# A decoder layer on one core: batches outermost and unrolled, with projection, norms and feed-forward placed between the attention steps

## The chip, the cores and the metric

One core of a Trainium2 chip, one launch. The metric is device time in microseconds from start to end of an execution, as the median of several runs. Beside it stands the span of one profiled execution, from its first to its last instruction.

## The reference

Four batches of 256 tokens, 256 channels, 16 heads of 128, float32. Three blocks follow one another, each with a residual and a layer norm without weights:

```python
q, k, v = x @ Wq, x @ Wk, x @ Wv                  # (4, 256, 16, 128) each
q, k = rmsnorm(q) * q_w, rmsnorm(k) * k_w
s = q k^T / sqrt(128) - slope[h] * (i - j)        # causal, slope[h] = 2 ** (-(h + 1) / 2)
y = rmsnorm(softmax(s) @ v) * sub_w               # per head
x = layernorm(x + concat(y) @ Wproj)              # (2048, 256)

a = softmax((ctx @ Wq.T + bq) (ctx @ Wk.T + bk)^T)  # (4, 256, 256), ctx has 128 channels
x = layernorm(x + x @ a^T)                        # over the channels of x

h = sigmoid(Q(x) @ Tg^T) * (Q(x) @ Tu^T)          # Tg, Tu, Td: ternary weights times their mean
x = layernorm(x + Q(h) @ Td^T)                    # Q: 8 bits per token; width 1024
```

## The kernel before

The tokens stand in tiles of 128, two per batch, eight in all (`NT`). Each engine runs its own list of instructions, and semaphores order them against one another; an engine never passes a waiting instruction of its own. The order of the work is written out by hand, the same way on each engine.

Prologue. SyncE issues all loads (L232 to L245). TensorE turns the cross-attention weights, the context and x, projects context queries and keys (L396) and forms the energies (L405). ScalarE and VectorE split the turned x into a high and a low part (`xT_hi` L596, `xT_lo` L720), so that three single-pass matmuls give a full-precision product. GpSimd does the same to the weights of the first two heads (`split`, L272 to L280: `w_hi` and `w_lo`, three pieces of 256 columns).

Attention. `attention_steps` (L206) runs 64 steps, one head of one batch in each, batches innermost: eight unrolled, then a loop of seven trips of eight (`Fori`). The weights of a head are therefore loaded and split once and used for four steps. A step works on several heads at once, as a pipeline: QKV of step n for tile 0 (L482), transposes of q and k of n-1 (L493), transposes of the probabilities of n-2 (L499), QKV of tile 1, scores of n-1 (L505, L506), values of n-2 (L512 to L514), transposes of y of n-3 (L521). The chain of one tile goes from QKV to squares (ScalarE, L635), sums (VectorE, L797), power -1/2 (GpSimd, L315), norm (VectorE, L791) and the transposes. QKV writes one PSUM bank per tile, so the next QKV of a tile waits for its norm. In some steps a piece of feed-forward weights is made ternary (`quantise_ff`, L777 to L782) and turned (L462), and in steps 3 to 6 the cross attention of a batch is normed and turned (L449). The turned y of all 64 heads stays in `yT`.

Tail. Only then the heads are projected: `project` (L422) accumulates 16 heads of a tile. The first two tiles fill the gaps of the last steps (`project_early`), the others those of a loop over tiles (L535 on), which does for a tile: residual and norm (L876), transposes (L550), cross attention (L557), norm, 8-bit quantisation (L900 to L904), gate and up (L587), sigmoid (L703), product (L865), quantisation of the hidden (L886 to L895, ScalarE L694), transposes (L564), down (L572), residual and norm (L908), store. Two neighbouring tiles overlap.

Of the kernel before, what the change touches and what calls it, by code (L numbers as in the profile page):

```python
# [40 lines left out]

def decoder_kernel(nc, x, ctx_in, wq, wk, wv, wproj, q_rms, k_rms, subln, xwq, xbq, xwk, xbk,
# [23 lines left out]
    ctx = ExitStack()
    with ctx:
# [3 lines left out]
        def sem(name):  # L71
# [6 lines left out]
        w_raw = sb("w_raw", [P, 2, KC, 3, D])  # L78
        w_hi = sb("w_hi", [P, 2, KC * 3 * D], F32R)
        w_lo = sb("w_lo", [P, 2, KC * 3 * D], F32R)  # L80
        bias = sb("bias", [P, 2, 3 * P])
        wp = sb("wp", [P, H, C])
        yT = sb("yT", [P, STEPS, T])
# [17 lines left out]
        v_sb = sb("v_sb", [P, B, TT, VW])  # L101
        y_n = sb("y_n", [P, TT, D])


        prep = yT[:].rearrange("p n t -> p (n t)")
        ctx_sb = prep[:, 0:NT * CC].rearrange("p (n c) -> p n c", n=NT)
        ctxT = prep[:, 1024:1024 + B * T]
        qcT = prep[:, 2048:2048 + B * T]
        kcT = prep[:, 3072:3072 + B * T]
        xw_sb = prep[:, 4096:4096 + 2 * CC].rearrange("p (a c) -> p a c", a=2)  # L110
        xwT = prep[:, 4352:4352 + 2 * CC].rearrange("p (a c) -> p a c", a=2)
        attn_sum = prep[:, 4608:4608 + NT]
        abs_w = prep[:, 5120:5120 + F]
        attn_raw = prep[:, 11264:11264 + NT * T].rearrange("p (n t) -> p n t", n=NT)
        attn = sb("attn", [P, NT, T])
        neg_xmax = sb("neg_xmax", [P, NT])
# [4 lines left out]
        ff_round = sb("ff_round", [P, C])  # L121
        ff_q = sb("ff_q", [P, C], BF16)
        w_sum = sb("w_sum", [P, 6])
        w_total = sb("w_total", [P, 3])
        w_scale = sb("w_scale", [P, 3])
        w_inv = sb("w_inv", [P, 3])


        res = sb("res", [P, 3, C])
        stats = sb("stats", [P, 3, nc.vector.BN_STATS_DIM])  # L130
        mean_var = sb("mean_var", [P, 3, 2])
        var_eps = sb("var_eps", [P, 3])
        ln_rstd = sb("ln_rstd", [P, 3])
        x1 = sb("x1", [P, C])
# [3 lines left out]
        x_most, x_scale, x_inv, h_most, h_scale, h_inv, down_scale = (sb(n, [P, 1]) for n in (  # L138
            "x_most", "x_scale", "x_inv", "h_most", "h_scale", "h_inv", "down_scale"))
        gate_up_scale = sb("gate_up_scale", [P, 2])  # L140
        round_col, table = sb("round_col", [P, 1]), sb("table", [P, 1])
        x_round = sb("x_round", [P, C])
        xq = sb("xq", [P, C], BF16)
        xqT = sb("xqT", [P, KC, P], BF16)

        sig, hid, h_round = ff_raw[:, 0, 0:F], ff_raw[:, 0, F:2 * F], ff_raw[:, 1, 0:F]
        hq = sb("hq", [P, F], BF16)
        hT = sb("hT", [P, FC, P], BF16)

# [7 lines left out]
        ps_yT = ps[:, 6, 0:T]  # L157
# [3 lines left out]
        s_vec, s_ctx, s_xw, s_wp = (sem(n) for n in ("vecs_loaded", "ctx_loaded", "xw_loaded", "wp_loaded"))  # L161
        s_ff = [sem("w_gate_loaded"), sem("w_up_loaded"), sem("w_down_loaded")]
        s_wraw = [sem("w_raw_even_loaded"), sem("w_raw_odd_loaded")]
        s_const, s_split_hi, s_split, s_bias, s_vecs = (sem(n) for n in (
            "constants_set", "w_hi_split", "w_lo_split", "bias_set", "vecs_scaled"))
        s_xT, s_xhi, s_xlo = sem("x_turned"), sem("xT_hi_set"), sem("xT_lo_set")
        s_cp = [sem("ctx_queries_projected"), sem("ctx_keys_projected")]
        s_ct, s_ctc, s_qcb, s_kcb, s_en, s_xmax, s_xexp, s_attn = (sem(n) for n in (
            "ctx_turned", "ctxT_copied", "ctx_queries_biased", "ctx_keys_biased", "energies_done", "energies_max",
            "energies_exp", "cross_attention_set"))  # L170
        s_at, s_atc = sem("cross_attention_turned"), sem("cross_attention_copied")
        s_wabs_act = sem("ff_abs_summed_by_scalar")
        s_wabs, s_wsum, s_wsc, s_wr, s_wq, s_wt, s_wtc = (sem(n) for n in (
            "ff_abs_summed", "ff_abs_total", "ff_scales_set", "ff_rounded", "ff_quantised", "ff_turned", "ff_turned_copied"))
# [7 lines left out]
        s_tqk, s_qkT, s_s, s_sc, s_p, s_tp, s_pT, s_y, s_sqy, s_ssy, s_yn, s_ty, s_yT = (sem(n) for n in (  # L182
            "qk_turned", "qkT_copied", "scores_done", "scores_biased", "probs_done", "probs_turned",
            "pT_copied", "y_done", "y_squared", "y_summed", "y_normed", "y_turned", "yT_copied"))
# [3 lines left out]
        (s_o, s_t1, s_x1T, s_xm, s_xq, s_gus, s_tq, s_xqT, s_gate, s_up, s_sig, s_hid, s_hs, s_hr, s_hq, s_th, s_hT,  # L188
         s_dn) = (sem(n) for n in (
             "projected", "x1_turned", "x1T_copied", "cross_mixed", "x2_quantised", "gate_up_scale_set", "xq_turned",  # L190
             "xqT_copied", "gate_done", "up_done", "sigmoid_done", "hidden_done", "hidden_scale_set",
             "hidden_rounded", "hidden_quantised", "hidden_turned", "hT_copied", "down_done"))
# [8 lines left out]
        def wait(eng, semaphore, count):  # L201

            if not isinstance(count, int) or count > 0:
                eng.wait_ge(semaphore, count)

        def attention_steps(eng, step, depth):  # L206

            for j in range(PAIR):  # L210
                step(j, j // B, j, lambda k, n=j: n >= k, 0)
            with eng.Fori(1, TRIPS) as trip:
                for j in range(PAIR):
                    step(trip * PAIR + j, trip * 2 + j // B, j, lambda k: True, trip)
            for n in range(STEPS, STEPS + depth):
                step(n, n // B, n % PAIR, lambda k, n=n: n - k < STEPS, TRIPS)

# [4 lines left out]
        def _(sp):  # L222
            def load_w(h, r):
                for a in range(3):
                    sp.dma_start(w_raw[:, r, :, a, :], w_d[a][:, :, bass.ds(h * D, D)]).then_inc(s_wraw[r], 16)
# [5 lines left out]

            sp.dma_start(xw_sb[:, 0, :], xwq).then_inc(s_xw, 16)  # L232
            sp.dma_start(xw_sb[:, 1, :], xwk).then_inc(s_xw, 16)
            sp.dma_start(ctx_sb, ctx_in.rearrange("b (t p) c -> p (b t) c", p=P)).then_inc(s_ctx, 16)
            for n, (first, last) in enumerate(((0, 1), (1, B))):
                tiles = slice(TT * first, TT * last)
                sp.dma_start(x_sb[:, tiles, :], x_d[:, tiles, :]).then_inc(s_x[n], 16)
            load_w(0, 0)
            for n, v in ((3, xbq), (4, xbk), (0, q_rms), (1, k_rms), (2, subln)):
                sp.dma_start(vecs[:, n:n + 1], v.rearrange("(p a) -> p a", a=1)).then_inc(s_vec, 16)  # L240
            load_w(1, 1)
# [466 lines left out]
        def _(dve):  # L708
# [75 lines left out]
            def step(n, head, j, live, trip):  # L784
# [22 lines left out]
                if live(0):  # L807
                    sums(0)
# [124 lines left out]
```

## Time and profile before

| | us |
|---|---|
| median of 3 runs | 435.16 (434.38 to 435.76) |
| span of the profiled execution | 432.9 |
| TensorE matmul busy | 401.9 (93%) |
| TensorE weight load busy | 361.1 (83%) |
| VectorE busy | 327.7 (76%) |
| ScalarE busy | 254.4 (59%) |
| GpSimd busy | 220.2 (51%) |

The end of a matmul is modelled in these records, and matmuls overlap, so a busy TensorE is no measure of its pace: for that the starts of successive groups are to be compared. The share of an engine is a mean over stages that have different limits. An idle time in front of an instruction is put down to what released it.

### The profile page before, as it was taken

The numbers are of one execution on the slowest core, as the hardware profiler recorded it, in microseconds if no ns is written. First come the engines' busy times: TensorE is split into PE (matmuls) and PEld (weight loads), VectorE is DVE, ScalarE is ACT, GpSimd is POOL, SyncE is SP. The second block draws the span as 40 slices with busy tenths as digits, with TensorE's granted clock in tenths as the row PEclk, the third lists the DMA queues.
The fourth block names the chain that finished last, engine by engine and source line by source line (L and its number), as shares of the span: only waits on it lengthen the run. The fifth ranks groups of instructions, "written<-read, shape, count | busy, mean of one in ns | idle before, by whom it ended". The sixth has DMA issues, their size and how long they took to land.

```text
span 432.9 us, 9595 instructions
## 1 busy us (share of the span) xinstructions
PE 401.9 (93%) x2605; PEld 361.1 (83%) x2612; DVE 327.7 (76%) x1000; ACT 254.4 (59%) x750; POOL 220.2 (51%) x368
## 2 busy tenths in 40 slices
PE   4979999999999999999999999999999899999552
PEld 3668899999999999999999999999988677777321
DVE  0777987887797798788779779878822788888862
ACT  3486777677676776767767677676722333333321
POOL 3633667676675776767767677675501122222210
PEclk9999999999999999999999999999999999999965
DMA  8980010110101101011010110000000000000000
GB/s 223 316 251 2 2 36 3 38 37 0 36 0 36 36 0 36 0 36 36 0 36 0 36 36 0 0 0 0 0 2 0 2 0 15 12 14 12 13 14 24
DMA packets 21747, 14.52 MB, mean 34 GB/s; under 512 B 1760, under 2 KB 21472, under 8 KB 21728
## 3 DMA queue, kind: packets, MB, share of 16 engines
q1 hardware_dynamic: 21728, 14.29, 11.2%
q8 instruction: 9, 0.15, 0.2%
q14 instruction: 10, 0.08, 0.1%
HBM read 13.24 MB, written 1.05 MB: 33 GB/s over the span
## 4 chain that ended last, share of the span: by engine, by line
PE 86%; DVE 5%; ACT 4%; issue 2%; DMA 1%; POOL 1%; SPq 0%; POOLq 0%; DVEq 0%
PE ps L482 30%; PE ps L422 11%; PE ps L493 7%; PE ps L506 6%; PE ps L499 5%; PE ps L512 4%; PE ps L505 3%; PE ps L514 3%; PE ps L513 3%; PE ps L521 3%; PE ps L587 3%; PE ps L572 2%; ACT hT L696 2%; DMA x_sb<-in_x 1%; PE ps L557 1%
## 5 line engine op out<-in xcount | busy, mean ns | idle before, releaser
L315 POOL TENSOR_TENSOR qk_rstd<-qk_sum,minus_half 128x2 f32<-128x2 f32 x128 | 88.5, 692 | 92.6 <-DVE qk_sum L797 90.8
L482 PE MATMUL ps<-w_hi,xT_hi 128*128 128x384 f32 x256 | 96.9, 378 | 2.3 <-DVE qk_n L791 1.4
L482 PE MATMUL ps<-w_hi,xT_lo 128*128 128x384 f32 x256 | 86.5, 338 | 0.0
L482 PE MATMUL ps<-w_lo,xT_hi 128*128 128x384 f32 x256 | 86.3, 337 | 0.0
L797 DVE TENSOR_REDUCE qk_sum<-sq 128x2 f32<-128x258 f32 x128 | 53.6, 419 | 30.8 <-ACT sq L635 29.1
L635 ACT ACTIVATE sq<-ps 128x256 f32<-128x256 f32 x128 | 49.1, 384 | 34.6 <-PE ps L482 34.4
L791 DVE TENSOR_TENSOR qk_n<-ps,qk_rstd 128x256 f32<-128x256 f32 x128 | 54.2, 423 | 18.8 <-POOL qk_rstd L315 17.8
L422 PE MATMUL ps<-wp,yT 128*128 128x256 f32 x256 | 62.2, 382 | 0.0
L310 POOL TENSOR_TENSOR y_rstd<-y_sum,minus_half 128x2 f32<-128x2 f32 x64 | 49.0, 766 | 24.6 <-DVE y_sum L804 20.9
L673 ACT ACTIVATE sqy<-ps 128x258 f32<-128x258 f32 x64 | 24.8, 387 | 58.5 <-PE ps L514 58.5
L422 PEld LDWEIGHTS ps<-wp,yT 128*128 128x128 f32 x256 | 46.7, 190 | 5.9
L482 PEld LDWEIGHTS ps<-w_hi,xT_hi 128*128 128x128 f32 x256 | 48.4, 189 | 3.0 <-DVE qk_n L791 1.7
L482 PEld LDWEIGHTS ps<-w_lo,xT_hi 128*128 128x128 f32 x256 | 48.6, 190 | 0.0
L482 PEld LDWEIGHTS ps<-w_hi,xT_lo 128*128 128x128 f32 x256 | 48.0, 188 | 0.0
L352 POOL TENSOR_SCALAR var_eps<-mean_var 128x1 f32<-128x1 f32 x24 | 7.0, 292 | 79.6 <-DVE mean_var L846 79.6
L835 DVE CUSTOM_DVE_ANT_0 score<-ps,bias 128x128 f32<-128x128 f32 (+1 forms) x128 | 40.3, 352 | 2.8 <-PE ps L506 2.8
L493 PE MATMUL ps<-ident,qk_n 128*128 128x128 f32 x256 | 38.7, 273 | 0.8 <-DVE qk_n L791 0.6
L506 PE MATMUL ps<-kT,qT 128*128 128x256 f32 x128 | 38.2, 380 | 0.0
L280 POOL TENSOR_TENSOR w_lo<-w_raw,w_hi 128x256 fp32r<-128x256 f32 x48 | 35.4, 738 | 4.0
L817 DVE COPY pT<-ps 128x384 f32<-128x384 f32 x64 | 35.1, 548 | 2.6 <-PE ps L499 2.5
L493 PEld LDWEIGHTS ps<-ident,qk_n 128*128 128x128 f32 x256 | 31.1, 140 | 5.0 <-issue 3.2
L639 ACT COPY v_sb<-ps 128x128 f32<-128x128 f32 x128 | 34.0, 266 | 0.0
(126 smaller groups left out, 846.9 us busy)
## 6 DMA issues: line engine op xcount, KB each, us to landing
w_raw<-in_L_attn_Wq SPq DMA_DIRECT2D x16, 128.0 KB, 2.2
w_raw<-in_L_attn_Wk SPq DMA_DIRECT2D x16, 128.0 KB, 2.3
w_raw<-in_L_attn_Wv SPq DMA_DIRECT2D x16, 128.0 KB, 2.3
wp<-in_L_attn_Wproj SPq DMA_DIRECT2D x1, 2048.0 KB, 16.1
ff_raw<-in_L_ffn_w_gate SPq DMA_DIRECT2D x1, 1024.0 KB, 8.6
ff_raw<-in_L_ffn_w_up SPq DMA_DIRECT2D x1, 1024.0 KB, 11.0
ff_raw<-in_L_ffn_w_down SPq DMA_DIRECT2D x1, 1024.0 KB, 13.0
out<-fin SPq DMA_DIRECT2D x8, 128.0 KB, 1.7
```

The source lines that it names most:

```text
L280: pool.tensor_tensor(lo, raw, hi, ALU.subtract).then_inc(s_split, 1)
L310: pool.tensor_tensor(y_rstd[:], y_sum[:], minus_half[:], ALU.pow).then_inc(s_ry, 1)
L315: pool.tensor_tensor(qk_rstd[:, t, :], qk_sum[:, t, :], minus_half[:], ALU.pow).then_inc(s_rs[t], 1)
L422: last = pe.matmul(ps[:, u % 2, 0:C], yT[:, h * B + b, t * P:(t + 1) * P], wp[:, h, :], start=(h == 0), stop=(h == H - 1))
L482: last = pe.matmul(ps[:, t, 0:3 * D], xa[:, k, tok], wa[:, r, k * 3 * D:(k + 1) * 3 * D], start=(i == 0), stop=(i == len(parts) - 1))
L493: last = pe.transpose(dst[:, t * P:(t + 1) * P], qk_n[:, t, a, :], ident[:])
L506: pe.matmul(ps_s[:, S1], qT[:, P:T], kT[:], start=True, stop=True).then_inc(s_s, 1)
L635: act.activation(sq[:, t, :, 0:D], ps[:, t, 0:2 * D].rearrange("p (a d) -> p a d", a=2), ACT.Square).then_inc(s_sq[t], 1)
L791: dve.tensor_tensor(qk_n[:, t], ps[:, t, 0:2 * D].rearrange("p (a d) -> p a d", a=2), r, ALU.mult).then_inc(s_qkn[t], 1)
L797: dve.tensor_reduce(qk_sum[:, t, :], sq[:, t], AX.X, ALU.add).then_inc(s_ss[t], 1)
L817: dve.tensor_copy(pT[:], ps_pT).then_inc(s_pT, 1)
L835: last = dve.tensor_tensor_reduce(score[:, s], ps_s[:, s], bias[:, r, s], 1.0, 3e38, ALU.add, ALU.min, neg_max[:, t:t + 1])
```

## The change

The order of the 64 steps becomes batch outermost: step n is head n % 16 of batch n // 16, and all steps are unrolled (plain Python loops, no `Fori`). What follows from it and comes with it:

- Each head is projected in step n+4 (`ps_o`, one PSUM bank that accumulates 16 heads of both tiles of a batch); `yT` keeps three heads, and its PSUM target moves into the bank of `ps_pT`.
- The weights are needed once per batch. The high part is made by ScalarE (`w_hi`, 768 columns in one instruction), the low part by GpSimd in three pieces (for the first two heads by VectorE), both for head n+2 in step n. Four heads stay in SBUF, the other twelve are written to DRAM (`w_store`) and read back in each later batch through four slots.
- All other work on TensorE becomes pieces ("fillers") at two places of a step: "a" behind the transposes of the probabilities, "b" at the end. `filler_plan` lists them: cross weights and context (XW, CT, CQ, CK), energies (EN), turned attention (AT), x of the other batches (XT), feed-forward weights (WS, FF, now twelve units of twice the size) in the steps of batch 0; and for each batch, in steps 0 to 11 behind its last projection, X (turn x1), M (cross attention), Q (turn quantised x), G0, G1, U0, U1 (gate, up), H (turn hidden), D (down) of its two tiles. They share one PSUM bank, and six after the last head.
- The sigmoid becomes a tanh with halved scale; the bias per head becomes one distance tile with the slope as a factor, and kT is scaled by its inverse.
- Loads start with x of batch 0 and head 0.

The diff, cut to its core:

```diff
+def filler_plan(batches, heads):
+    plan = [(1, "a", "XW", 0), (1, "b", "CT", 0), (2, "a", "CT", 1), (2, "b", "CQ", 0), (3, "a", "CK", 0),
+            (4, "a", "EN", 0), (4, "b", "WS", 0), (5, "a", "AT", 0), (5, "b", "XT", 1), (6, "a", "EN", 1),
+            (7, "a", "AT", 1), (8, "a", "CQ", 1), (9, "a", "CK", 1), (10, "a", "EN", 2), (11, "a", "AT", 2),
+            (12, "a", "EN", 3), (13, "a", "AT", 3), (14, "a", "XT", 2), (15, "a", "XT", 3)]
+    plan += [(FF_STEP + i, "b", "FF", i) for i in range(12)]
+    tail = [(1, "a", "X", 0), (1, "b", "M", 0), (2, "a", "X", 1), (2, "b", "M", 1), (3, "b", "Q", 0),
+            (4, "a", "G0", 0), (4, "b", "U0", 0), (5, "a", "G1", 0), (5, "b", "U1", 0), (6, "a", "Q", 1),
+            (6, "b", "G0", 1), (7, "a", "U0", 1), (7, "b", "G1", 1), (8, "a", "U1", 1), (8, "b", "H", 0),
+            (9, "a", "D", 0), (10, "a", "H", 1), (10, "b", "D", 1)]
+    for b in range(batches):
+        plan += [(heads * (b + 1) + 4 + s, slot, kind, 2 * b + t) for s, slot, kind, t in tail]
...
 # SyncE
+            sp.dma_start(x_sb[:, 0:TT, :], x_d[:, 0:TT, :]).then_inc(s_x[0], 16)
+            load_w(0)
             sp.dma_start(xw_sb[:, 0, :], xwq).then_inc(s_xw, 16)
             sp.dma_start(xw_sb[:, 1, :], xwk).then_inc(s_xw, 16)
+            load_w(1)
             sp.dma_start(ctx_sb, ctx_in.rearrange("b (t p) c -> p (b t) c", p=P)).then_inc(s_ctx, 16)
+            load_w(2)
+            load_w(3)
...
+            for b in range(1, B):
+                for h in range(KEPT, H):
+                    reload_w(b * H + h)
...
 # GpSimd
+            def split_lo(h, piece):
+                cols = slice(piece * KC * D, (piece + 1) * KC * D)
+                if piece == 0:
+                    pool.wait_ge(s_hi, h + 1)
...
+            for n in range(LAST):
+                live = [k <= n < STEPS + k for k in range(5)]
+                b, s = (n - 4) // H - 1, (n - 4) % H
+                if live[3]:
                     pool.wait_ge(s_ssy, n - 2)
                     wait(pool, s_yn, n - 3)
                     pool.tensor_tensor(y_rstd[:], y_sum[:], minus_half[:], ALU.pow).then_inc(s_ry, 1)
+                if n < H - LEAD:
+                    split_lo(n + LEAD, 0)
+                if live[0]:
+                    qk_pow(0, n)
+                if n < H - LEAD:
+                    split_lo(n + LEAD, 1)
+                    split_lo(n + LEAD, 2)
...
+                if live[0]:
+                    qk_pow(1, n)
...
 # TensorE, end of a step
+                if live[4]:
+                    m = n - 4
+                    b, h = m // H, m % H
+                    pe.wait_ge(s_yT, m + 1)
...
+                    for t in range(TT):
+                        last = pe.matmul(ps_o[:, t, :], yT[:, m % 3, t * P:(t + 1) * P], wp[:, h, :],
+                                         start=(h == 0 and t == 0), stop=(h == H - 1), skip_group_check=True)
+                    last.then_inc(s_pj, 1)
+                filler(n, "b")
...
 # ScalarE
+            def w_hi(h):
+                act.wait_ge(s_wraw[h % RAW], 48 * (h // RAW + 1))
+                if h >= KEPT + RING:
+                    act.wait_ge(s_stored[place(h) - KEPT], 16 * ((h - KEPT) // RING))
+                    act.wait_ge(s_qkv[1], h - RING + 1)
+                act.copy(w_hl[:, place(h), 0, :], w_raw[:, h % RAW].rearrange("p k a d -> p (k a d)")).then_inc(s_hi, 1)
...
+                    act.activation(qT[:], ps_qT, ACT.Copy, scale=qk_scale)
+                    act.activation(kT[:], ps_kT, ACT.Copy, scale=1.0 / SLOPE[(n - 1) % H]).then_inc(s_qkT, 1)
+                consume(n, "a")
+                if n < H - LEAD:
+                    w_hi(n + LEAD)
+                if live[0]:
+                    squares(1, n)
...
 # VectorE, a step
+                consume(n - 1, "b")
+                if 0 <= ff < 12:
+                    unround_ff(ff)
+                if (n - 1, "a") in PLAN and PLAN[n - 1, "a"][0] == "EN":
+                    norm_cross(PLAN[n - 1, "a"][1])
+                if s == 0:
+                    residual0(A)
...
                     norm(0, n)
+                consume(n, "a")
+                if 0 <= ff < 12:
+                    quantise_ff(ff)
+                if s == 0:
+                    residual0(A2)
+                if s == 3:
+                    quantise_x(A)
+                if s == 4:
+                    quantise_x(A2)
+                if live[0]:
+                    sums(1, n)
...
+                if 1 <= n < 4:
+                    sum_ff(n - 1)
+                if 0 <= ff + 1 < 12:
+                    scale_ff(ff + 1)
```

## Rows read from the trace of the kernel before

**Rows 1.** busy time by stage: count, granted clock, DMA share, GB/s at the end

```profile
0.00:18.77 18.77, 13.21 (x50) 9.32 (x51) 5.83 (x12) 7.08 (x13) 10.13 (x30) 1.00 0.90 251
18.77:60.93 42.16, 37.58 (x248) 33.79 (x247) 33.98 (x99) 30.54 (x97) 18.56 (x28) 1.00 0.32 101
60.93:310.70 249.77, 249.77 (x1759) 240.49 (x1759) 205.98 (x671) 175.39 (x576) 167.86 (x258) 1.00 0.06 18
310.70:404.00 93.30, 89.36 (x498) 71.17 (x502) 65.92 (x181) 33.09 (x55) 19.60 (x43) 1.00 0.02 8
404.00:433.00 29.00, 11.98 (x55) 6.37 (x56) 15.95 (x40) 8.26 (x11) 4.04 (x10) 0.69 0.04 14
```

**Rows 2.** timeline of TensorE, one steady step: start, length, line, tiles, count

```profile
150.88 0.60 PE L493 MATMUL ps<-ident,qk_n 128*128 128x128 f32 x4
...
154.16 0.42 PE L482 MATMUL ps<-w_hi,xT_hi 128*128 128x384 f32 x1
...
155.30 0.60 PE L493 MATMUL ps<-ident,qk_n 128*128 128x128 f32 x4
```

**Rows 3.** timeline of TensorE, early projection and the start of two tiles

```profile
312.38 2.76 PE L422 MATMUL ps<-wp,yT 128*128 128x256 f32 x12
...
314.97 0.60 PE L493 MATMUL ps<-ident,qk_n 128*128 128x128 f32 x4
...
384.28 1.89 PE L422 MATMUL ps<-wp,yT 128*128 128x256 f32 x8
...
395.20 1.89 PE L422 MATMUL ps<-wp,yT 128*128 128x256 f32 x8
```

**Rows 4.** timelines of TensorE and GpSimd in the first 11 us, with releasers

```profile
5.97 1.97 PE L388 MATMUL ps<-ident,yT 128*128 128x128 f32 x8 [1.97 <-DMA yT<-in_ctx]
...
10.63 0.41 POOL L276 TENSOR_SCALAR w_hi<-w_raw 128x256 fp32r<-128x256 f32 x1 [6.01 <-DMA w_raw<-in_L_attn_Wv]
```

**Rows 5.** ScalarE: timeline of one step, then groups (x count, busy us, mean ns)

```profile
155.97 0.50 ACT L661 ACTIVATE qT<-ps,vecs 128x256 f32<-128x256 f32 x1
...
156.34 0.40 ACT L662 COPY kT<-ps 128x256 f32<-128x256 f32 x1
...
L624 ACT ACTIVATE yT<-ff_raw 128x1024 f32<-128x1024 f32 x3 | 3.2, 1073 | 0.0
...
L609 ACT ACTIVATE yT<-ps,vecs 128x512 f32<-128x512 f32 x2 | 1.4, 688 | 3.1 <-PE ps L396 3.0
```

**Rows 6.** costliest groups of the page, GpSimd (busy us, mean ns, idle before)

```profile
L315 POOL TENSOR_TENSOR qk_rstd<-qk_sum,minus_half 128x2 f32<-128x2 f32 x128 | 88.5, 692 | 92.6 <-DVE qk_sum L797 90.8
...
L280 POOL TENSOR_TENSOR w_lo<-w_raw,w_hi 128x256 fp32r<-128x256 f32 x48 | 35.4, 738 | 4.0
```

**Rows 7.** VectorE: timeline of one step, then groups by form

```profile
153.32 0.42 DVE L797 TENSOR_REDUCE qk_sum<-sq 128x2 f32<-128x258 f32 x1
...
154.54 0.42 DVE L791 TENSOR_TENSOR qk_n<-ps,qk_rstd 128x256 f32<-128x256 f32 x1 [0.25 <-POOL qk_rstd L315]
...
L727 DVE TENSOR_REDUCE w_sum<-ff_raw 128x1 f32<-128x1024 f32 x3 | 3.6, 1212 | 0.0
...
L746 DVE TENSOR_REDUCE neg_xmax<-ps 128x2 f32<-128x512 f32 x4 | 2.5, 683 | 0.0
...
L779 DVE TENSOR_SCALAR ff_round<-ff_round 128x256 f32<-128x256 f32 x24 | 7.1, 295 | 0.8
```

**Rows 8.** timeline of GpSimd, the power for y in two steps

```profile
151.04 0.70 POOL L310 TENSOR_TENSOR y_rstd<-y_sum,minus_half 128x2 f32<-128x2 f32 x1 [0.46 <-DVE y_sum L804]
...
155.67 0.89 POOL L310 TENSOR_TENSOR y_rstd<-y_sum,minus_half 128x2 f32<-128x2 f32 x1
```

**Rows 9.** timeline of VectorE, first and last of the last tile

```profile
404.91 0.39 DVE L876 TENSOR_TENSOR res<-ps,x_sb 128x256 f32<-128x256 f32 x1
...
430.25 0.41 DVE L851 TENSOR_SCALAR fin<-res,mean_var,ln_rstd 128x256 f32<-128x256 f32 x1 [1.02 <-POOL ln_rstd L355]
```

**Rows 10.** DMA issues of the page: count, KB each, us to landing

```profile
out<-fin SPq DMA_DIRECT2D x8, 128.0 KB, 1.7
```

More of the change, by code:

```diff
@@ L201, in wait, with await_filled, await_read, place @@
         def wait(eng, semaphore, count):
-            if not isinstance(count, int) or count > 0:
+            if count > 0:
                 eng.wait_ge(semaphore, count)
[L206 to L216, printed above, removed]
+        def await_filled(eng, kind, arg):
+            eng.wait_ge(s_fill, USE[kind, arg][0] + 1)
+        def await_read(eng, kind, arg):
+            _, bank, before = USE[kind, arg]
+            eng.wait_ge(s_read[bank], before + 1)
+        def place(h):
+            return h if h < KEPT else KEPT + (h - KEPT) % RING
         block = ctx.enter_context(nc.Block())
@@ L297, in _ @@
-            for r in range(2):
-                pool.wait_ge(s_wraw[r], 48)
-                for piece in range(SPLITS):
-                    parts = split(r, piece)
-                    pool.wait_ge(s_split_hi, r * SPLITS + piece + 1)
-                    split_lo(*parts)
-            def step(n, j, live, before=None):
-                if before:
-                    pool.wait_ge(*before)
-                if live(3):
+            pool.iota(dist[:, S0], pattern=[[-1, P]], base=0, channel_multiplier=1,
+                      allow_small_or_imprecise_dtypes=True).then_inc(s_dist, 1)
@@ L358, in _ @@
[L358 to L363 removed]
+                if n < H - LEAD:
[5 more added lines that the diff above has]
+                    split_lo(n + LEAD, 2)
+                if b >= 0 and s == 0:
+                    ln_pow(0, 2 * b)
@@ new lines, in filler @@
+                    last = pe.matmul(dst[:, 0:6], ones[:], w_sum[:], start=True, stop=True)
+                if kind == "EN":
+                    await_read(pe, "CQ", arg // 2)
+                    await_read(pe, "CK", arg // 2)
+                    tok = arg % 2 * T
+                    for i in range(TT):
+                        last = pe.matmul(dst[:, i * T:(i + 1) * T], qcT[:, tok + i * P:tok + (i + 1) * P],
+                                         kcT[:, tok:tok + T], start=True, stop=True)
@@ new lines, in filler @@
+                if kind == "H":
+                    pe.wait_ge(s_hq, arg + 1)
+                    for f in range(FC):
+                        last = pe.transpose(turned[:, f * P:(f + 1) * P], hq[:, f * P:(f + 1) * P], ident16[:])
+                if kind == "D":
+                    await_read(pe, "H", arg)
+                    for f in range(FC):
+                        last = pe.matmul(dst[:, 0:C], hT[:, f, :], wdT[:, f, :], start=(f == 0), stop=(f == FC - 1))
+                last.then_inc(s_fill, 1)
@@ L488, in step @@
+            for n in range(LAST):
+                live = [k <= n < STEPS + k for k in range(5)]
+                if live[0]:
+                    qkv(0, n)
+                if live[1]:
                     for t in range(TT):
@@ L615, in exponentials @@
+            w_hi(0)
+            w_hi(1)
+            def exponentials(b, bank):
                 act.wait_ge(s_xmax, b + 1)
```

1041 lines of the change are left out of this document (517 added, 524 removed).

## Prediction

> **What bounds the kernel now.** I first read the busy time by stages, to see where TensorE is not fed, then TensorE's own timeline in those stages, then one step on each other engine. By stages [rows 1]: before the first head's projection TensorE works 13.2 of 18.8 us, from 60.9 to 310.7 us it is busy without a gap, in the tail to 404 us it lacks 3.9 of 93.3 us, and in the last 29 us it works 12.0, at a mean granted clock of 0.69, so partly at 1.2 GHz. The first four steps hide another 4.6 us of idle time. All told 31 of 432.9 us are idle: no change of order can save more unless a busy TensorE is also not at its pace. Its pace in a steady step: the transposes of q and k start at 150.88 and again at 155.30, so a step is 4.42 us, and there is no idle entry between [rows 2]. Six QKV matmuls take 1.14 of it up to the transposes (154.16 to 155.30), and six more follow; the rest is transposes, scores and values.
>
> The other engines in that step: VectorE's instructions are some 3.3 us long in 4.42 (206 busy of 249.8 us with the feed-forward pieces), ScalarE 3.1, GpSimd 3.0 [rows 1]. None bounds, but they form one chain: squares on ScalarE, sums on VectorE, power on GpSimd, norm on VectorE, transposes.
>
> **The part that moves without changing in sum.** Projecting a head in its own step puts two 128x256 fp32 products there. Six took 314.97-312.38 = 2.59 us, 0.432 each [rows 3]: the step becomes 4.42+0.865 = 5.285 us. A tile's other work on TensorE comes from the tail: from one tile to the next 10.92 us, of which 14 projections are 6.05, so at most 4.87 us are left, with the waits of that loop among them [rows 3]. I take 4.5 (4.87 would be 2.2 us more in the sum): three batches, six tiles, 26.9 us, now lie between heads.
>
> **Start.** The first head no longer stands behind the cross attention: x of batch 0 and head 0 are the first 0.65 MB, as the cross weights and the context were before, which were there at 5.97 [rows 4]; with rounding on ScalarE and the low part on VectorE the first projection can start near 7.9 instead of 18.8. But the loop order takes much of it back. GpSimd's step is now: power for y, first third of the low part of head n+2, power for tile 0, the other two thirds, power for tile 1. The first third waits for `w_hi(n+2)`, which ScalarE does in the same step n behind the copies of qT and kT and the copy of filler "a". Queued behind that wait are both powers, so both norms, and with the second norm the transposes of the next step. In step 0 `w_hi(2)` needs the third head's weights, 2.1 MB into the queue; the same 2.1 MB stood ahead of 10.63 us before [rows 4]. So: rounding to 11.5, third 12.25, power 12.95, thirds 14.45, power 15.15, norm 15.6, transposes of step 1 at 15.65 (24.50 in the kernel before).
>
> **The chain in steps 1 to 13**, from the start of one step's transposes to that of the next. Transposes to qT 0.67 (155.30 to 155.97), qT and kT 0.74 (spacing 0.37) [rows 2, 5]. `w_hi` of 768 elements is not in the trace: 1024 take 1.07 and 256 take 0.50 [rows 5]; I take 0.85, in proportion, ends 0.50 and 1.07 (-5 and +3 us over 14 steps). It ends at 2.26. A third of the low part 0.74, power 0.69, spaced by 0.70 [rows 6]: power for tile 0 from 3.0 to 3.7, the thirds to 5.1, power for tile 1 to 5.85. Norm and hand-over 0.5 [rows 7]: 6.35. VectorE in its own order is as long: norm 0 at 3.75, 0.34; quantise a feed-forward piece 0.42 (256 elements 0.295, 512 not shown, ends 0.30 and 0.60); sums and the score reduction together 1.0 (153.32 to 154.54 less 0.25 idle); scale the next piece 0.45; norm 1 0.47: 6.44 [rows 7]. What filler "a" adds: EN, a maximum on VectorE (0.68, spaced 0.63 [rows 7]): 7.07; CQ 7.2; CK, 0.87 us on TensorE and a 0.69 us copy ahead of `w_hi` [rows 5]: 7.48; AT, which waits for VectorE's normalisation of the attention (ready 1.5 us after the mark) and is copied ahead of `w_hi`: 7.73. Steps 4 and 5, without feed-forward pieces, 6.35 and 7.22. Steps 4 to 13 together: 6.35+7.22+3x7.07+3x7.73+7.2+7.48 = 72.65 us. TensorE alone needs 10x5.285 and 10 us of fillers, 62.9: so 9.8 us of new waiting. Steps 1 to 3: the same chain plus VectorE's 1.21 us sums of the feed-forward weights [rows 7], less the pieces: 7.15+7.24+7.74 = 22.1, where TensorE needs 14.6: 7.5 us.
>
> GpSimd's instructions can also be held by VectorE's: the power for y takes 0.70 alone and 0.89 beside VectorE's rounding of a feed-forward piece [rows 8]. Eight steps x 0.2 us are 1.6 us, inside the range. The Trainium skill (SBUF — State Buffer, "Who interferes with whom") says that a GpSimd instruction and a VectorE instruction in a 2-port mode, tensor_scalar among them, exclude each other for the whole instruction. By that rule a third could wait out a 512-element piece: 8x3x0.45 = 10.8 us if every piece met one. The row shows 0.2, so I leave it out of the sum.
>
> **From step 14 on TensorE bounds.** No split is left. VectorE's work in the tail is 82 us for eight tiles [rows 1], 20 us a batch. It has 3.3 us plus at most 3.2 of a tile's work in a step of 5.4 to 6.4, and it starts 0.6 to 1 us ahead of TensorE, so its long steps (the two residuals of a batch; residual, quantising and norm together) cost at most a few tenths: nothing in the sum, up to 3.3 us a batch in the range. 49 steps to the last head: 259.0, two x turns 0.9, four feed-forward turns 1.0, six tiles 26.9: 287.8 us. Weights: batches 1 to 3 read 0.79 MB a step from the copy in DRAM, 149 GB/s; before, the first stage ran at 251 [rows 1]. The issue leads its use by three to four steps, 16 us or more; that cover is what hides it.
>
> **Drain and tail.** After the last QKV (1.96 us after the mark) the chain of the last head has no fill any more: squares to norm 2.1, transposes and copies 1.5, scores 0.9, reduction 0.7, exponentials 0.85, turn and copy 1.15, values 0.9, y's norm 2.1, turn, copy and projection 2.0: 12.2 us, an estimate from these instructions in a steady step, 0.3 to 0.7 us each [rows 2, 5 to 7], and 0.05 for each hand-over. Then the last two tiles alone. One tile took 404.91 to 430.25 and 2.6 us to the end of the span [rows 9], 28.0. Two tiles share each engine in a fixed order: x1 of the first at 2.7, M done 4.7 and 6.8, quantised x 9.9 and 12.0, gate and up done 14.1 (half clock) and 18.4, scale 16.5 and 21.2, first D at 22.9; the second tile's quantised hidden stands behind the first's last residual on VectorE, 24.7, then turn, copy and D 28.8, residual, power and norm 31.2, store 33.4. At full clock about 30.
>
> **Sum.** 15.65 + 22.1 + 72.65 + 287.8 + 1.96 + 12.2 + 33.4 = 445.8 us of span, beside 432.9 before. The median before is 435.16, 2.3 us above the span: 448 us.
>
> **Rivals.** (1) Faster: the chain through `w_hi` and the thirds is covered, because thirds, rounding and norms pack closer than I space them. It decides at 6.0 to 6.45 us a step, TensorE's own need. For it: I add full hand-overs, and my step is only 0.4 to 1.7 us longer. Against it: the order on ScalarE and GpSimd is fixed, and ends are known durations. Price: 448-7.5-9.8 = 431 us; with the tail at full clock 428. (2) Batch boundaries: VectorE's extra 20 us a batch does not fit beside the heads; 3x3.3 us more, 458. For it: 3.3+3.2 us in the fourth tail step against 5.4. Against: VectorE's lead. (3) The ring of four weight slots: `w_hi(8)` and later wait for the store of the head four before. At 128 KB in 1.7 us, as an output store takes [rows 10], a store would be 10.2 us and each of eight steps 4 us longer: 480. Against: that time is mostly fixed cost, and the first store is due only at 53 us, when some 10.5 MB are through at 251 GB/s by 42.
>
> **Chances.** Forecast 0.60, rival 1 0.19, rival 2 0.15, rival 3 0.06. A difference under 0.3% (433.9 to 436.5) is about what a measurement of this kernel cannot tell from none; it takes 0.04 of rival 1 and 0.03 of the forecast's lower edge. So faster 0.15, same 0.07, slower 0.78. The range 432 to 460 holds the forecast with its bounds, the upper part of rival 1 and most of rival 2; outside are rival 3 and the lower half of rival 1, some 0.2.
>
> **What would show it.** Transposes of step 1 near 15.7 us; steps of 7 to 7.7 us up to the fourteenth and 5.3 after it; in those first steps GpSimd's first third waits for ScalarE's `w_hi`, and the second norm releases the transposes; between 110 and 398 us TensorE without gaps; from the last projection to the end some 33 us. It would be wrong if the first steps run at TensorE's 6 us, or if the later ones are much over 5.3.

## The result: 455.73 us, and the profile after

The changed kernel takes 455.73 us (455.02 to 455.92), the kernel before, run beside it, 435.05: a ratio of 1.0476, with a 95% interval of 1.0456 to 1.0497. The profiled span grew from 432.9 to 454.1 us. Forecast were 448 us of time and 445.8 of span, slower.

The first view is the busy time by stage, as in [rows 1]: count of us, then TensorE, weight load, VectorE, ScalarE, GpSimd, the granted clock, the DMA share and GB/s. The cuts are the starts of the transposes of q and k in step 1, 4, 14 and 63, and the end of the last projection.

```profile
0.00:16.74 16.74, 7.32 (x23) 6.25 (x23) 4.50 (x10) 5.35 (x9) 5.85 (x21) 1.00 0.84 246
16.74:38.91 22.17, 18.05 (x96) 14.96 (x95) 11.91 (x33) 15.03 (x40) 10.91 (x16) 1.00 1.03 327
38.91:115.01 76.10, 67.52 (x424) 57.06 (x425) 50.39 (x154) 49.62 (x140) 44.27 (x60) 1.00 0.39 142
115.01:404.43 289.42, 288.43 (x1922) 269.66 (x1932) 225.76 (x725) 183.55 (x534) 119.82 (x182) 1.00 0.31 104
404.43:419.80 15.37, 12.77 (x78) 10.21 (x76) 7.73 (x25) 6.57 (x19) 4.33 (x7) 1.00 0.03 9
419.80:454.10 34.30, 14.82 (x64) 8.03 (x64) 20.18 (x58) 8.57 (x12) 4.89 (x12) 0.70 0.02 8
```

Against the terms of the sum, in us of span:

| part | forecast | measured | difference |
|---|---|---|---|
| to the transposes of step 1 | 15.65 | 16.74 | +1.1 |
| steps 1 to 3 | 22.1 | 22.17 | +0.1 |
| steps 4 to 13 | 72.65 | 76.10 | +3.45 |
| steps 14 to 62 | 287.8 | 289.42 | +1.6 |
| last QKV and drain | 14.16 | 15.37 | +1.2 |
| last two tiles | 33.4 | 34.30 | +0.9 |

The place of the loss is the first 115 us. There TensorE is idle 9.4, 4.1 and 8.6 us; over the next 289 us it lacks 1.0. In the later steps its pace is what the forecast said: the timeline of TensorE shows two transposes of q and k 5.28 us apart, beside the 4.42 of [rows 2], as two more products per step ask.

```profile
143.80 0.60 PE L532 MATMUL ps<-ident,qk_n 128*128 128x128 f32 x4
...
149.08 0.60 PE L532 MATMUL ps<-ident,qk_n 128*128 128x128 f32 x4
```

What a slow step waits for is seen in step 13, which turns the attention (AT) and a feed-forward piece. Its timeline on TensorE, ScalarE, GpSimd and VectorE, in this order (start, length, what; in brackets the idle time before and what ended it):

```profile
107.23 0.63 PE L532 MATMUL ps<-ident,qk_n 128*128 128x128 f32 x4
...
115.01 0.63 PE L532 MATMUL ps<-ident,qk_n 128*128 128x128 f32 x4 [0.23 <-issue]
...
109.40 0.59 ACT L621 COPY attn<-ps 128x512 f32<-128x512 f32 x1 [0.41 <-PE ps L462]
109.88 0.84 ACT L587 CAST w_hl<-w_raw 128x768 fp32r<-128x768 f32 x1
...
110.80 0.72 POOL L359 TENSOR_TENSOR w_hl<-w_raw,w_hl 128x256 fp32r<-128x256 f32 x1 [2.46 <-ACT w_hl L587]
111.48 0.69 POOL L378 TENSOR_TENSOR qk_rstd<-qk_sum,minus_half 128x2 f32<-128x2 f32 x1
112.13 1.59 POOL L359 TENSOR_TENSOR w_hl<-w_raw,w_hl 128x256 fp32r<-128x256 f32 x2
113.69 0.77 POOL L378 TENSOR_TENSOR qk_rstd<-qk_sum,minus_half 128x2 f32<-128x2 f32 x1
...
108.51 0.41 DVE L756 TENSOR_REDUCE qk_sum<-sq 128x2 f32<-128x258 f32 x1
...
112.20 0.42 DVE L750 TENSOR_TENSOR qk_n<-ps,qk_rstd 128x256 f32<-128x256 f32 x1 [2.48 <-POOL qk_rstd L378]
...
114.49 0.42 DVE L750 TENSOR_TENSOR qk_n<-ps,qk_rstd 128x256 f32<-128x256 f32 x1
```

The row of VectorE at 108.51 has the sums that the first power needs; they are done at 108.9. But the power starts at 111.48, since GpSimd stands 2.46 us at the first third, which wants ScalarE's rounding of the weights, which stands behind the copy of AT. Then come 1.6 us of thirds between the two powers, the second norm at 114.49, and 0.5 us later the next transposes. Over the whole run the waits add up as follows (total us, times, longest):

```profile
DVE qk_n L750 <- POOL qk_rstd L378: 40.1, 37, 3.3
POOL w_hl L359 <- ACT w_hl L587: 38.5, 14, 9.3
```

Steps 4 to 13 last 8.23, 7.02, 7.12, 7.80, 7.47, 7.96, 7.46, 7.79, 7.47 and 7.78 us. Against the forecast of each, 1.9 of the 3.45 us too many are in step 4 alone, and 1.65 in steps 8 to 13. Step 4 shows another wait. VectorE, ScalarE, then TensorE:

```profile
42.53 0.42 DVE L750 TENSOR_TENSOR qk_n<-ps,qk_rstd 128x256 f32<-128x256 f32 x1 [1.71 <-POOL qk_rstd L378]
...
43.59 0.47 ACT L598 ACTIVATE attn_raw<-ps,neg_xmax 128x256 f32<-128x256 f32 x1 [1.24 <-DVE neg_xmax L881]
...
44.51 1.05 ACT L653 ACTIVATE attn<-ff_raw 128x1024 f32<-128x1024 f32 x1
...
45.79 0.36 PE L450 MATMUL ps<-w_sum,ones 128*128 128x6 f32 x2 [1.61 <-ACT attn L653]
```

The filler WS needs ScalarE's third sum over the feed-forward weights; that is queued behind the exponentials of EN, those wait for VectorE's maximum (42.88, not shown), that stands behind the first norm, and the norm waits for the power behind the first third. TensorE waits 1.61 us, and QKV and the transposes at 47.14, which follow WS on its list, wait with it.

### The profile page after: what moved, and what is told of

It is laid out like the page before. It is cut to its first block, busy times and chain, and to the rows that moved or that the text cites. A ratio compares the mean times of both kernels' runs of the same rounds, so it can differ in the third digit from the quotient of the medians.

```text
span 454.1 us, 9089 instructions
## 1 busy us (share of the span) xinstructions
PE 408.9 (90%) x2602; PEld 366.2 (81%) x2612; DVE 320.5 (71%) x1002; ACT 268.7 (59%) x752; POOL 190.1 (42%) x298
## 2 busy tenths in 40 slices
DMA packets 28736, 52.62 MB, mean 116 GB/s; under 512 B 2576, under 2 KB 22288, under 8 KB 28688
## 4 chain that ended last, share of the span: by engine, by line
PE 68%; issue 11%; POOL 10%; DVE 6%; ACT 2%; SPq 1%; DMA 1%; POOLq 0%; DVEq 0%; ACTq 0%
PE ps L518 23%; PE ps L571 10%; PE ps L532 5%; PE ps L547 5%; PE ps L538 4%; POOL qk_rstd L378 4%; POOL w_hl L359 4%; PE ps L491 3%; PE ps L552 3%; PE ps L554 3%; PE ps L553 3%; PE ps L546 3%; PE ps L560 2%; POOL y_rstd L386 2%; PE ps L500 2%
## 5 line engine op out<-in xcount | busy, mean ns | idle before, releaser
L518 PE MATMUL ps<-w_hl,xT_hi 128*128 128x384 f32 x512 | 150.9, 376 | 6.3 <-DVE qk_n L750 3.6
L378 POOL TENSOR_TENSOR qk_rstd<-qk_sum,minus_half 128x2 f32<-128x2 f32 x128 | 92.5, 723 | 121.7 <-DVE qk_sum L756 121.3
L518 PEld LDWEIGHTS ps<-w_hl,xT_hi 128*128 128x128 f32 x512 | 91.6, 193 | 14.8 <-issue 9.8
L518 PE MATMUL ps<-w_hl,xT_lo 128*128 128x384 f32 x256 | 87.8, 343 | 0.0
L518 PEld LDWEIGHTS ps<-w_hl,xT_lo 128*128 128x128 f32 x256 | 49.2, 192 | 0.0
L359 POOL TENSOR_TENSOR w_hl<-w_raw,w_hl 128x256 fp32r<-128x256 f32 x42 | 30.7, 746 | 38.5 <-ACT w_hl L587 38.5
L532 PEld LDWEIGHTS ps<-ident,qk_n 128*128 128x128 f32 x256 | 30.4, 141 | 11.9 <-issue 10.1
L677 ACT ACTIVATE prob<-score,neg_max 128x128 f32<-128x128 f32 x64 | 25.5, 398 | 20.9 <-DVE neg_max L954 20.9
L538 PE MATMUL ps<-ident,prob 128*128 128x128 f32 x192 | 31.9, 275 | 2.4 <-ACT yT L683 2.1
L689 ACT ACTIVATE qT<-ps,vecs 128x256 f32<-128x256 f32 x64 | 30.9, 482 | 2.7 <-PE ps L532 2.6
L678 ACT ACTIVATE prob<-score,neg_max 128x256 f32<-128x256 f32 x64 | 31.8, 497 | 0.0
```

The costliest lines, as they stand in the source:

```text
L359: pool.tensor_tensor(w_hl[:, place(h), 1, cols], raw, w_hl[:, place(h), 0, cols].bitcast(F32), ALU.subtract).then_inc(s_lo, 1)
L378: pool.tensor_tensor(qk_rstd[:, t, :], qk_sum[:, t, :], minus_half[:], ALU.pow).then_inc(s_rs[t], 1)
L518: last = pe.matmul(ps[:, t, 0:3 * D], xa[:, k, tok], w_hl[:, place(h), wa, k * 3 * D:(k + 1) * 3 * D], start=(i == 0), stop=(i == len(part ...
L532: last = pe.transpose(dst[:, t * P:(t + 1) * P], qk_n[:, t, a, :], ident[:])
L538: last = pe.transpose(ps_pT[:, i * P:(i + 1) * P], prob[:, i * P:(i + 1) * P], ident[:])
```

## The experiments

The theory: GpSimd's order is the loss. The powers wait behind the first third, and so for ScalarE's rounding. Its rivals: the length of the thirds, the traffic of the weights through DRAM, and VectorE's load at the ends of the batches.

**All thirds behind both powers.**

```diff
-                if n < H - LEAD:
-                    split_lo(n + LEAD, 0)
                 if live[0]:
                     qk_pow(0, n)
-                if n < H - LEAD:
-                    split_lo(n + LEAD, 1)
-                    split_lo(n + LEAD, 2)
...
                 if live[0]:
                     qk_pow(1, n)
+                if n < H - LEAD:
+                    for piece in range(SPLITS):
+                        split_lo(n + LEAD, piece)
```

> One edit to the changed kernel: GpSimd's three thirds of the low part stand behind both powers of the step instead of around the first. Chain theory (the thirds and their wait for ScalarE's w_hi hold the second norm): the steps from the first to the fourteenth transposes, 98.3 us in the changed kernel, fall to what TensorE needs there, 77.5 us, if nothing else takes over: down to 435; with part of it kept by VectorE's sums of the feed-forward weights and a late start 434 to 440. Rival (batch 0 is long because VectorE and ScalarE have more work there: rounding, exponentials, feed-forward pieces): the powers come earlier but the norms do not, at least 450 of the 455.7 us stay.

Measured: 436.06 us (434.88 to 436.55), ratio to before 1.0012 (0.9984 to 1.0040). The same AT step, on TensorE and GpSimd:

```profile
90.10 0.60 PE L530 MATMUL ps<-ident,qk_n 128*128 128x128 f32 x4
...
96.47 0.60 PE L530 MATMUL ps<-ident,qk_n 128*128 128x128 f32 x4
...
91.59 0.69 POOL L378 TENSOR_TENSOR qk_rstd<-qk_sum,minus_half 128x2 f32<-128x2 f32 x1
94.03 0.91 POOL L378 TENSOR_TENSOR qk_rstd<-qk_sum,minus_half 128x2 f32<-128x2 f32 x1 [1.74 <-DVE qk_sum L754]
94.68 2.37 POOL L359 TENSOR_TENSOR w_hl<-w_raw,w_hl 128x256 fp32r<-128x256 f32 x3
```

The step is 6.37 us instead of 7.78, and steps 4 to 13 take 64.5 instead of 76.1, where 62.9 had been worked out as TensorE's own need. The first power now follows its sums, and the thirds run behind both. The move is worth 19.7 us. So the order is the cause, with the wait that it puts ahead of the powers; the next two runs tell the wait from the length of the thirds.

**Only the first power ahead of the thirds.** The three thirds stand between the two powers.

> All three thirds stand between the two powers: only the first power is freed. Chain theory: the first norm comes early, the second stands behind 2.1 us of thirds that begin when w_hi is done, 0.7 us earlier than in the changed kernel; VectorE's branch behind the first norm no longer counts. About 0.8 to 1.2 us a step over 13 steps: 440 to 446. If only the first norm mattered, it would be as fast as with both powers first. Rival (VectorE and ScalarE's work): 450 or more.

Measured: 440.75 us (439.91 to 442.38), ratio 1.0128 (1.0097 to 1.0159). Most of the loss, 15.0 of 19.7 us, belongs to what stands ahead of the first power; 4.7 us belong to the thirds between the two.

**The order as changed, but the rounding a step earlier on ScalarE**, so that its result lies ready when GpSimd gets to the first third. This tells the wait from the length of the thirds.

```diff
-                if n < H - LEAD:
-                    w_hi(n + LEAD)
+                if n == 0:
+                    w_hi(LEAD)
+                elif n + LEAD + 1 < H:
+                    w_hi(n + LEAD + 1)
                 if live[0]:
                     squares(1, n)
+                if n == 0:
+                    w_hi(LEAD + 1)
```

> GpSimd's order stays as changed, but ScalarE makes w_hi one step earlier, so that the first third finds it done. Tells the wait from the length of the thirds: if the wait for w_hi is what holds the powers, 434 to 441, as with both powers first; if it is the 2.1 us that the thirds take on GpSimd, 448 or more.

Measured: 438.80 us (437.08 to 440.36), ratio 1.0078 (1.0043 to 1.0113). GpSimd's order is untouched, and its wait for the rounding shrinks to one, in the first step, where the weights are not there sooner:

```profile
POOL w_hl L359 <- ACT w_hl L587: 9.3, 1, 9.3
```

Steps 4 to 13 take 63.2 us, 1.3 less than in the first edit. So the thirds themselves can stand ahead of the powers in these steps at no cost that shows; what cost 16.9 us was that the first of them waits. The 2.7 us by which this run is behind the first edit lie at the start, where the one wait is left: the transposes of step 1 start at 16.77 instead of 14.71, and steps 1 to 3 take 19.97 us instead of 17.24.

**No store and no reload of the weights**, and no waits for them (TensorE's and ScalarE's, not in the lines below).

```diff
-                if h - RAW >= KEPT:
-                    store_w(h - RAW)
-            for h in range(H - RAW, H):
-                store_w(h)
...
-                    reload_w(b * H + h)
```

> Leaves out the copy of the weights to DRAM and the reading back, so that batches 1 to 3 multiply with whatever heads lie in the four slots; the instructions of the engines stay. Chain theory: the reload is hidden, 455.7 within 1 us. Rival (38 MB of weight traffic is what slows it, by contention or waits): 450 or less.

Measured: 457.09 us (455.25 to 458.52), ratio 1.0497 (1.0459 to 1.0534), no gain. That is 1.4 us over the changed kernel where 1 was allowed for, with ranges that overlap; a cause for it is not shown. The page of the changed kernel has these transfers (KB each, us to landing):

```profile
w_hl<-w_store SPq DMA_DIRECT2D x36, 768.0 KB, 4.3
w_store<-w_hl SPq DMA_DIRECT2D x12, 768.0 KB, 4.0
```

A reload lands after 4.3 us, and in the trace of the changed kernel TensorE waits for none of them; the whole traffic, 52.62 MB instead of 14.86 without it, is hidden.

**The clock of the tail**, on top of the first edit: in the gaps of the last two tiles TensorE turns the identity into a free bank, with no reader.

```diff
+                if n > STEPS + 4:
+                    warm({"X": 4, "M": 16 * t, "Q": 4, "U1": 16 * t, "H": 8, "D": 12 * (1 - t)}.get(kind, 0))
+            def warm(count):
+                for _ in range(count):
+                    pe.transpose(ps[:, 4, 0:P], ident[:], ident[:])
...
+                    if n == STEPS + 3:
+                        warm(20)
```

> The kernel with both powers first (436.06 us), and after the last head extra transposes of the identity where TensorE waits for others (20 behind the last projection, 4 to 16 behind the pieces of the last two tiles), into a bank that nothing reads. They do no work; they keep TensorE active. In the changed kernel the last 35 us ran at a mean granted clock of 0.71. If the price of the half clock in the exposed tail is real (products M, H and D of the second tile about twice as long on the chain): 2 to 3 us less, 433 to 434.5. Rival (the tail is the other engines' latency, the clock costs nothing): 436 within 0.7, or more if the extra transposes delay the real ones.

Measured: 433.23 us (432.66 to 434.76), ratio 0.9964 (0.9948 to 0.9980), 2.8 us under the first edit alone. The window of the tail (columns as above) and the down projection of the last tile on TensorE's timeline, first with the first edit alone:

```profile
400.50:434.70 34.20, 15.40 (x67) 7.71 (x65) 20.20 (x58) 8.63 (x12) 4.91 (x12) 0.67 0.02 8
...
428.00 1.87 PE L498 MATMUL ps<-wdT,hT 128*128 128x256 bf16 x8 [1.19 <-ACT hT L646]
```

Then with the extra transposes:

```profile
400.00:432.30 32.30, 22.45 (x168) 17.38 (x166) 20.11 (x58) 8.90 (x13) 4.90 (x12) 0.95 0.03 9
...
426.41 1.03 PE L498 MATMUL ps<-wdT,hT 128*128 128x256 bf16 x8 [0.31 <-ACT hT L655]
```

At a mean granted clock of 0.67 the engine spends two thirds of the stretch at its lower level, 1.2 GHz, and eight matmuls take 1.87 us; at 0.95 they take 1.03. The two windows are not cut at the same point of the work: from the start of the last projection (399.05 and 399.70) to the end of the span it is 35.65 us without the transposes and 32.60 with them, 3.05 less.

**The same in the kernel before**, where the last 29 us ran at 0.69 [rows 1], and nothing else changed.

> The kernel before, with nothing but extra transposes of the identity into a free bank in the gaps of its last tile, as in the run with the tail's clock. It tells how much of what the best reordered version won belongs to the new order at all. In the last tile of before, gate took 1.82 us for four matmuls, the hidden's transposes 1.03 and down 1.89, where at full clock they take about 1.0, 0.6 and 1.0. If the half clock has the same price here, some 3 us, the time is 432 to 433 us, and the new order with everything repaired stands level with the old one treated alike. If the price belongs to the changed kernel's two-tile tail alone, 434.5 to 436 us.

Measured: 431.97 us (430.70 to 432.23), ratio 0.9948 (0.9935 to 0.9961). The window of its tail, to be read beside the last line of [rows 1]:

```profile
404.00:428.90 24.90, 15.48 (x119) 11.71 (x119) 15.42 (x39) 7.78 (x10) 4.03 (x10) 0.93 0.05 17
```

So the clock of the tail is worth 2 to 3 us in either order of the steps. And the old order with it is as fast as the best version of the new one, below: 0.9948 and 0.9937 of before, with intervals that overlap.

**The start**, on top of the first edit: rounding behind both squares on ScalarE, and VectorE's sums of the feed-forward weights one step later, behind a norm.

```diff
-                if n < H - LEAD:
-                    w_hi(n + LEAD)
                 if live[0]:
                     squares(1, n)
+                if n < H - LEAD:
+                    w_hi(n + LEAD)
...
+                if 2 <= n < 5:
+                    sum_ff(n - 2)
...
-                if 1 <= n < 4:
-                    sum_ff(n - 1)
```

> The kernel with both powers first, and two shifts in batch 0: ScalarE does w_hi behind both tiles' squares instead of between them, and VectorE's three sums of the feed-forward weights lie behind the norm of tile 0 in steps 2 to 4 instead of at the end of steps 1 to 3, where the second norm stood behind them. By the chain theory what is left of batch 0 above TensorE's own need is in steps 1 to 4 (24.1 us, own need about 21): 2 to 4 us less, 432 to 434. Rival (TensorE bounds everywhere after the powers are freed): 436 within 0.7.

Measured: 437.37 us (434.92 to 437.92), ratio 1.0047 (1.0028 to 1.0066): no gain, the expectation missed. The trace is that of the shortest execution, 434.92. Steps 1 to 3 did get shorter, 4.24, 5.51 and 6.09 us instead of 5.27, 5.60 and 6.37, but step 4 took 7.92 instead of 6.90, and step 14 begins at 96.27 us, where the first edit has 96.47. I put that down to the sum that was moved into it, and tested it below.

**All parts together**: the first edit, the transposes of the identity in the tail and 20 more before the first head, the edits of the start, and the last tile's hidden layer quantised ahead of the residual of the tile before it.

> Both powers first, the shifts in batch 0, the extra transposes in the tail, 20 more before and behind the first turn of x, so that the first projections meet the full clock, and in the last two tiles the second tile's hidden quantised ahead of the first tile's last residual on VectorE (1.3 us earlier). If each gains what the traces say (2 to 3 in the tail, 2 to 4 and about 1 at the start, 1.3): 427 to 431, below both kernels. If the tail and the start are bound by other engines: 434 to 436.

Measured: 431.73 us (431.23 to 433.36), ratio 0.9937 (0.9914 to 0.9960). It is 0.6% under the kernel before and 24 us under the changed one, but misses the 427 to 431 expected of all the gains together.

**The same without the moved sums.**

> The version with all parts put together, less one of them: VectorE's three sums of the feed-forward weights stay at the end of steps 1 to 3; ScalarE's rounding still stands behind both squares. If the moved sums are what made the step of 7.92 us (fourth to fifth), the first four steps keep part of their gain and the step is 6.9 us again: 430 to 431 us. If the early gain itself came from the moved sums, the steps are 5.3, 5.6, 6.4 and 6.9 us again and the time is 431.5 to 432.5 us, as with them.

Measured: 432.57 us (431.69 to 434.15), ratio 0.9963 (0.9942 to 0.9985). Neither expectation came true: steps 1 to 3 stay short in part (5.01, 5.52, 6.02), and step 4 is still 8.03 us. The moved sums are not the reason for it. TensorE at WS in this kernel, and ScalarE's sum before it:

```profile
37.50 0.36 PE L452 MATMUL ps<-w_sum,ones 128*128 128x6 f32 x2 [1.01 <-ACT attn L664]
...
36.20 1.07 ACT L664 ACTIVATE attn<-ff_raw 128x1024 f32<-128x1024 f32 x1
```

The same two in the first edit:

```profile
37.49 0.36 PE L448 MATMUL ps<-w_sum,ones 128*128 128x6 f32 x2 [0.27 <-ACT attn L651]
...
36.19 1.07 ACT L651 ACTIVATE attn<-ff_raw 128x1024 f32<-128x1024 f32 x1
```

ScalarE's third sum starts at 36.19 or 36.20 us in both, although step 4 began at 31.95 in the first edit and at 30.81 here. In this kernel the rounding (34.55, 0.85 us long) stands just ahead of the exponentials and that sum; in the first edit it was done before the squares. So TensorE's early lead is lost at WS, at the same wait as in the changed kernel: the start is bound there by ScalarE's list. In the run of the start alone, with the sums moved as well, TensorE waits 1.00 us at WS for the same sum. Whether moving VectorE's sums alone, or WS a step later, would keep the lead was not tried.

## Why the prediction was right, point by point

**The direction and its cause** hold as put: steps over 7 us up to the fourteenth, GpSimd at `w_hi`, the second norm as the releaser of the transposes, 5.28 us afterwards. The order of GpSimd's list was known from the diff, and the durations from the trace of before; that was enough to find a loss which no share of busy time shows (GpSimd is busy 42%). The sum was still 8.3 us of span short, and no error made up for another: all six terms came out long.

**The first transposes**, +1.1 us: the rounding of the third head ended at 12.60 instead of 11.5, because its weights arrived at 11.77, while [rows 4] had the same number of bytes through before 10.63. From there each step of that chain held.

**Steps 1 to 3**, 22.17 for 22.1, and **steps 4 to 13**, +3.45 us. The estimate of `w_hi`, 0.85, was measured at 0.83 to 0.86. The step that failed is "Steps 4 and 5, without feed-forward pieces, 6.35 and 7.22": step 4 was costed along VectorE and GpSimd only, and ScalarE's own list, with EN's exponentials and the third sum ahead of WS, was left out. 1.9 us are lost there. The second miss is what was left out of the sum and kept for the range, the collisions of GpSimd and VectorE at 1.6 us: the eight steps with a feed-forward piece, 6 to 13, are 1.8 us over the forecast together. The quantising of a piece was taken at 0.42 us and took this (x count, then shortest, median and longest in ns):

```profile
L785 DVE TENSOR_SCALAR ff_q<-ff_round x12: 415/594/685, 58.7 to 135.1; 128x512 bf16<-128x512 f32 x12
```

The eight pieces of steps 6 to 13 took 0.59 to 0.69 us, the four behind them, with no third beside them, 0.41 to 0.42. Eight times some 0.2 us is near the 1.8, but that is a match of sums: in steps 7, 11 and 13, where the attention is turned, the pieces took 0.59 too and the steps are only 0.05 to 0.07 us over; in steps 8, 10 and 12, 0.27 to 0.40 over, the second power took 0.91 us in place of 0.69 as well. How the 1.8 us divide is not shown.

The rule of the Trainium skill (SBUF — State Buffer, "Who interferes with whom"), that the later of the two is blocked until the earlier has ended, would have asked for 10.8 us by the prediction's estimate, in which every piece meets every third. The trace shows 0.17 to 0.27 us a piece, so the smaller price was nearer; it does not speak against the rule, since a piece that starts late in a third has only the rest of it to wait for.

**Steps 14 to 62**, +1.6 us: with the new waits gone this stretch is TensorE's, as said. Of the 1.6, 1.3 are the size of a tile's own work: the ten steps from 154.36 to 216.60 us, which carry the two tiles of a batch, are 9.4 us over ten of 5.28, so 4.7 a tile where 4.5 was taken, between the ends named; six tiles make 1.3.

**Drain and tail**, +2.1 us of 47.6. In the drain ScalarE's own list was left out once more: the last head's probabilities are turned at 413.42, 1.30 us after its exponentials began where 0.85 was taken, because the copy of an earlier head's turned y stands behind them on ScalarE, and the turn waits for that copy, which empties the bank that the two share:

```profile
412.81 0.46 ACT L683 ACTIVATE yT<-ps,vecs 128x256 f32<-128x256 f32 x1
...
413.42 0.52 PE L538 MATMUL ps<-ident,prob 128*128 128x128 f32 x3 [0.53 <-ACT yT L683]
```

That is 0.45 of the 1.2 us; another 0.25 is lost ahead of the exponentials, which begin behind the squares for another head's y (411.84, not shown). The tail's 0.9 us are there when M is done: 5.4 and 7.9 us after the last projection, where 4.7 and 6.8 were forecast. Its four matmuls took 1.88 and 1.55 us; in the run with the extra transposes they take 1.13. The first of them, in the changed kernel and in that run:

```profile
423.36 1.88 PE L479 MATMUL ps<-attn,x1T 128*128 128x256 f32 x4 [0.46 <-ACT x1T L636]
...
405.12 1.13 PE L477 MATMUL ps<-attn,x1T 128*128 128x256 f32 x4
```

The forecast names the half clock at gate and up only.

**Rival 1** (the chain is covered, 431 us) fell for this kernel, but the first experiment made it nearly true: 436.06. What it still lacks is spread: steps 1 to 3 at 17.24 rather than 14.6, steps 4 to 13 at 64.5 rather than 62.9, and the terms above that were sized too small. **Rival 2** (VectorE at the batch ends, 458) was near in time and wrong in cause: TensorE works 288.4 of 289.4 us in that stretch. **Rival 3** (the ring waits for stores, 480) is denied: a store of 768 KB lands in 4.0 us, not in the 10.2 worked out from small ones, and leaving it out gained nothing.

**Why even the repaired order gains nothing.** Saved is idle TensorE time only, and that was 31 us. The first edit has 434.7 - 402.2 = 32.5 us of it: 10.8 up to step 14 and 21.4 from 384.90 on. In the kernel before the start had 10.1 and the tail with the last 29 us 21.0 [rows 1]. Starting 9.8 us earlier (the first transposes at 14.71 instead of 24.50) only moves the cross attention behind them, as fillers. What the new order could hide, the old one had hidden for the most part with the projections of the other tiles; what neither hides, a pipeline that fills at the start and runs dry at the end, is of the same length in both.

## What to carry to other kernels

When an instruction with a late input is put on an in-order engine, cost it by what stands behind it there: one third of 0.7 us, that waits 2.75 us in the mean and holds up a power, cost 15 us over 14 steps; with its input ready ahead of time it cost nothing that shows in steps 4 to 13. Follow every engine's list through a step, also of those that look idle; the one left out (ScalarE ahead of WS) was the largest single miss here, and later took back the gain of another edit. Before a reordering is built, add up the idle time of the bounding engine stage by stage and ask which of it the new order can reach: here, with the powers first, 32.5 us were idle where 31 had been, while useless extra work in the tail's gaps brought 2 to 3 us in either order.

## What the runs showed of the hardware

**The pace of TensorE at the start.** In the changed kernel the QKV matmuls start 0.32 us apart up to 20 us and 0.17 apart from 21.65 on, although the granted clock stands at 1.00 for the whole stretch in the windows. With 20 transposes of the identity ahead of them the same matmuls start 0.17 us apart. TensorE in the changed kernel:

```profile
7.97 0.98 PE L518 MATMUL ps<-w_hl,xT_hi 128*128 128x384 f32 x2 [2.69 <-DVE w_hl L737]
8.74 0.52 PE L518 MATMUL ps<-w_hl,xT_lo 128*128 128x384 f32 x1
9.06 0.84 PE L518 MATMUL ps<-w_hl,xT_hi 128*128 128x384 f32 x2
```

And with all parts together:

```profile
7.81 0.58 PE L527 MATMUL ps<-w_hl,xT_hi 128*128 128x384 f32 x2 [0.25 <-DVE w_hl L748]
8.23 0.34 PE L527 MATMUL ps<-w_hl,xT_lo 128*128 128x384 f32 x1
8.41 0.52 PE L527 MATMUL ps<-w_hl,xT_hi 128*128 128x384 f32 x2
```

In the first case the engine had been idle up to 4.19 us and again for 2.69 us, in the second it had worked since 2.16 us with hardly a gap. That the slow pace is the lower clock shows in the run without the reload, where the column does fall at the start: after 3.54 us of idle time it stands at 0.50, that is at 1.2 GHz, and the same matmuls start 0.32 us apart (window as above, then TensorE):

```profile
14.50:18.00 3.50, 2.97 (x11) 2.74 (x12) 1.39 (x4) 0.54 (x2) 1.97 (x3) 0.50 1.00 328
...
15.81 0.52 PE L511 MATMUL ps<-w_hl,xT_lo 128*128 128x384 f32 x1
16.13 0.84 PE L511 MATMUL ps<-w_hl,xT_hi 128*128 128x384 f32 x2
```

So the column can stand at 1.00 at the start while the spacing says 1.2 GHz. The Trainium skill (TensorE: Matmul & The Clock Gate, "Part 1: The HAM clock gate") has the slow clock as the default which work releases, and these traces agree: 0.32 us without work ahead, 0.17 with it.

**GpSimd and VectorE slow one another.** In the first edit the rounding of a piece took 0.83 us (0.42 in the changed kernel at 107.38), the normalisation of the attention 1.03 (0.69 there at 107.90), and the power for y 1.14 (0.70 in [rows 8]), where they met:

```profile
89.11 0.83 DVE L777 TENSOR_SCALAR ff_round<-ff_round 128x512 f32<-128x512 f32 x1
...
90.05 1.03 DVE L761 TENSOR_TENSOR attn_raw<-attn_raw,attn_sum 128x512 f32<-128x512 f32 x1
...
89.61 0.92 POOL L359 TENSOR_TENSOR w_hl<-w_raw,w_hl 128x256 fp32r<-128x256 f32 x1
90.49 1.14 POOL L386 TENSOR_TENSOR y_rstd<-y_sum,minus_half 128x2 f32<-128x2 f32 x1
```

That is 0.34 to 0.44 us more each, about twice the 0.2 of [rows 8]. TensorE was the later one in these steps (63.55 busy of 64.52 us), so they cost little.
